# Second layer of a two-layer megakernel: three edits to its slot tables (decay loads, tile stores, the chain to the next batch's time steps)

## What is computed

```
xn = layernorm(x);  h = rmsnorm(xn)
u, z = split(h @ in_proj);  u = silu(conv4(u))
dt_r, B, C = split(u @ x_proj)
dt = softplus(dt_r @ dt_proj + b);  A = -exp(A_log)         # 256 channels x 16 states
state[t] = exp(dt[t] * A) * state[t-1] + dt[t] * B[t] * u[t]
y = (sum over states of C[t] * state[t] + u * D) * silu(z)
x + xn + y @ out_proj + (shared(xn) + top-2 of 8 experts(xn)) / 3
```

## Time and profile before

| | us |
|---|---|
| three runs | 1224.32, 1230.9, 1238.44 |
| their median | 1230.9 |
| profiled execution, its own time | 1228.28 |
| profiled execution, span from first to last instruction | 1226.5 |

### The profile page before, as it was taken

The page is one execution under the profiler, slowest core; times in us unless marked ns, Lnnn a source line. Parts: engine busy times, 40 slices in busy tenths (PEclk is TensorE's granted clock), DMA queues, the critical chain, the costliest instruction groups (busy, mean ns, idle before and its releaser), DMA issues. The chain is left out here.

```text
span 1226.5 us, 12808 instructions
## 1 busy us (share of the span) xinstructions
PE 871.2 (71%) x3620; PEld 412.1 (34%) x3620; DVE 938.6 (77%) x1280; ACT 505.5 (41%) x840; POOL 701.0 (57%) x427
## 2 busy tenths in 40 slices
PE   3668988888888656676587687688777688664552
PEld 0123333333333323344244344344434344311120
DVE  3467787977977445799469879688979779899973
ACT  0112212123123322473376386385495485663230
POOL 1021122031113561379569877569989879789996
PEclk9568788788897867699689899797999889875575
DMA  4886746666450352767766766767877767646631
GB/s 127 208 180 144 187 140 153 184 171 152 118 142 14 99 155 63 155 145 165 185 196 176 188 207 167 158 215 172 207 217 169 182 207 174 206 141 126 163 86 28
DMA packets 102849, 192.30 MB, mean 157 GB/s; under 512 B 13147, under 2 KB 68124, under 8 KB 90364
## 3 DMA queue, kind: packets, MB, share of 16 engines
q1 hardware_dynamic: 91516, 183.07, 57.2%
q0 software_dynamic: 11264, 8.43, 4.2%
HBM read 146.80 MB, written 32.06 MB: 146 GB/s over the span
## 5 line engine op out<-in xcount | busy, mean ns | idle before, releaser
L1681 POOL TENSOR_TENSOR hs<-hs,c_rep 128x1024 f32<-128x1024 f32 x128 | 332.0, 2604 | 87.7 <-DVE hs L1931 86.9
L1922 DVE TENSOR_TENSOR p_s_du<-p_s_du,b_rep 128x512 f32<-128x512 f32 x256 | 175.4, 685 | 49.5 <-PE p_s_du L2029 46.2
L2029 PE MATMUL p_s_du<-block_in,spread 96*128 96x512 bf16 x256 | 112.9, 442 | 115.5 <-DVE hs L1931 109.0
L1931 DVE TENSOR_TENSOR_SCAN hs<-decays,p_s_du 128x512 f32<-128x512 f32 x132 | 161.1, 1221 | 13.5 <-DVE p_s_du L1922 0.5
L1931 DVE TENSOR_TENSOR_SCAN hs<-slots,p_s_du 128x512 f32<-128x512 f32 x100 | 122.1, 1221 | 19.7 <-ACT slots L1826 9.7
L802 DVE TENSOR_TENSOR value_prod<-p_eb_y_acc,v 128x512 f32<-128x512 f32 x128 | 83.9, 685 | 56.6 <-PE p_eb_y_acc L1109 47.1
L513 POOL TENSOR_TENSOR sc<-ex,ex_part 128x1024 f32<-128x1024 f32 x8 | 17.0, 2129 | 171.6 <-ACT ex_part L619 171.6
L1826 ACT ACTIVATE decays<-decays,a_neg 128x512 f32<-128x512 f32 x132 | 91.7, 718 | 49.4 <-DMA decays<-dt_rows 39.3
L1720 POOL DMA_INDIRECT y_xr<-moe_sums,position x64 | 105.4, 1647 | 10.8 <-issue 8.2
L1686 POOL TENSOR_TENSOR y_hid<-y_hid,g_in 128x512 f32<-128x512 f32 x64 | 99.0, 1548 | 20.3 <-DVE y_hid L1944 19.8
L2029 PEld LDWEIGHTS p_s_du<-block_in,spread 96*128 96x128 bf16 x256 | 26.1, 102 | 249.4 <-DVE hs L1931 179.0
(11 more groups left out here) (193 smaller groups left out, 1751.6 us busy)
## 6 DMA issues: line engine op xcount, KB each, us to landing
decays<-dt_rows SPq DMA_DIRECT2D x33, 1024.0 KB
qb<-rq_rows SPq DMA_DIRECT2D x32, 1024.0 KB, 13.5
slots<-dt_rows SPq DMA_DIRECT2D x25, 1024.0 KB
wm<-in_wmoe SPq DMA_DIRECT2D x48, 384.0 KB
moe_rows<-zeros SPq DMA_DIRECT2D x8, 774.0 KB, 6.0
xg<-moe_rows SPq DMA_DIRECT2D x48, 129.0 KB
stack<-ex_part SPq DMA_DIRECT2D x96, 64.0 KB
block_in<-y_part SPq DMA_DIRECT2D x192, 32.0 KB
```

What stands on the lines that cost most here:

```text
L1681: nc.gpsimd.tensor_tensor(hs[:, n:n + 2], hs[:, n:n + 2], c_rep[p][:].unsqueeze(1).to_broadcast([128, 2, T]), ALU.mult)\
L1922: nc.vector.tensor_tensor(p_du[:, k % 2], p_du[:, k % 2], b_rep[p][:], ALU.mult).then_inc(dbu_done.sem, 1)
L1931: nc.vector.tensor_tensor_scan(hs[:, n % NA], home(8 * (b - 1) + k // 4)[:, bass.ts(j, T)], p_du[:, k % 2], 0.0, ALU.mult, ALU.add).then_i ...
L2029: nc.tensor.matmul(p_du[:, k % 2], spread[:, i], block_in[:, (2 * b + s) % NB, j], start=True, stop=True).then_inc(du_full.sem, 1)
```

## The change

Four things in the slot tables of layer 1; no instruction is added or taken away.

- SP, decay loads: from batch 2 on at slots 0, 4, 8, 12, 16 in place of 2, 6, 10, 14, 18 (q 3 to 7), and for the next batch at 22, 24, 28 in place of 22, 26, 30 (q 0 to 2). In a slot they now come first, then weights, then rows (before: rows, weights, decays).
- SP, tile stores: two slots later (`store`).
- The chain: `x_proj` to `third_part` one slot sooner on PE and ACT, two for `log_in`, `softplus_cut`, `softplus_end` and `steps`, one for `store_dt`, `stack` (first half) and the parts. On POOL `steps` comes ahead of `times_c` and `hidden` of its slot, and `hidden` ahead of `times_c`. `repeat_bc` goes from slot 16 to 19.
- The end of the batch before: `gather_y` of its last four slots from PE slot 3 to 2; `out_proj` from 9 to 13 and `result` from 11 to 15 (batches 2 to 7).

```diff
-  weigh=then + 6 if h else then + 2, store=then + 8 if h else then + 4),
+  weigh=then + 6 if h else then + 2, store=then + 10 if h else then + 6),
 # sync, batch
+                if b == 1 and k in (4, 8, 12, 15, 18):
+                    load_decays(1, {4: 3, 8: 4, 12: 5, 15: 6, 18: 7}[k])
+                if 1 < b <= B and k % 4 == 0 and k < 20:
+                    load_decays(b, (k + 12) // 4)
+                if nxt and k in (22, 24, 28):
+                    load_decays(b + 1, (k - 20) // 4)
+                (weights, then rows)
-                (rows, then weights)
-                if b == 1 and k in (4, 8, 12, 15, 18):
-                    load_decays(1, {4: 3, 8: 4, 12: 5, 15: 6, 18: 7}[k])
-                if 1 < b <= B and k % 4 == 2 and k < 20:
-                    load_decays(b, (k + 10) // 4)
-                if nxt and k % 4 == 2 and k > 20:
-                    load_decays(b + 1, (k - 22) // 4)
-                    if k == 16:
+                    if k == 19:
                         repeat_bc(b + 1, 1 - p)
-                    if k in (19, 21):
-                        store_dt(b + 1, (k - 19) // 2)
-                    if k in (21, 23, 24):
-                        stack(b + 1, 0, (21, 23, 24).index(k))
+                    if k in (18, 20):
+                        store_dt(b + 1, (k - 18) // 2)
+                    if k in (20, 22, 23):
+                        stack(b + 1, 0, (20, 22, 23).index(k))
 # gpsimd, batch: both now ahead of times_c
+                if nxt and k in (16, 18):
+                    steps(b + 1, q, (k - 16) // 2)
+                for _, _, j, v in due(b, k, "hidden"):
+                    hidden(v)
-                if nxt and k in (18, 20):
-                    steps(b + 1, q, (k - 18) // 2)
 # scalar, batch
-  copy_xd 9, dt_in 11 13, exp_z 13, one_more 14, log_in 15, first_part 20 23, second_part 22 25
+  copy_xd 8, dt_in 10 12, exp_z 12, one_more 13, log_in 13, first_part 19 22, second_part 21 24
 # vector, batch
-  result 11, softplus_cut 16, softplus_end 17, second_rest 21 24, third_part 22 26
+  result 15 if nxt else 11, softplus_cut 14, softplus_end 15, second_rest 20 23, third_part 21 25
 # tensor, batch
-  x_proj 8, dt_proj 10 12, last gather_y 3, out_proj(b - 1, 1) 9
+  x_proj 7, dt_proj 9 11, last gather_y 2, out_proj(b - 1, 1) 13 if nxt else 9
```

More of the change, by code:

```diff
@@ L1610, in batch @@
                         load_xr(0)
+                if b == 1 and k in (4, 8, 12, 15, 18):
[4 more added lines that the diff above has]
+                    load_decays(b + 1, (k - 20) // 4)
+                for _, _, j, _ in due(b, k, "weights"):
+                    if j is not None:
+                        load_weights(j)
                 for _, _, j, _ in due(b, k, "rows"):
@@ L1613, in batch @@
                         load_rows(j)
-                for _, _, j, _ in due(b, k, "weights"):
-                    if j is not None:
-                        load_weights(j)
-                if b == 1 and k in (4, 8, 12, 15, 18):
-                    load_decays(1, {4: 3, 8: 4, 12: 5, 15: 6, 18: 7}[k])
-                if 1 < b <= B and k % 4 == 2 and k < 20:
-                    load_decays(b, (k + 10) // 4)
                 if b == 4 and k == 30:
                     load_xr(1)
-                if nxt and k % 4 == 2 and k > 20:
-                    load_decays(b + 1, (k - 22) // 4)
                 for _, _, j, _ in due(b, k, "store"):
@@ L1735, in batch @@
                     times_c(b, p, k // 2 - 1)
-                for _, _, j, v in due(b, k, "hidden"):
-                    hidden(v)
                 if old and k == 5:
@@ L1874, in batch @@
                     silu_z(b + 1, q)
-                if k == 9:
+                if k == 8:
                     copy_xd(b + 1)
-                if k in (11, 13):
-                    dt_in(b + 1, (k - 11) // 2)
+                if k in (10, 12):
+                    dt_in(b + 1, (k - 10) // 2)
+                if k == 12:
+                    exp_z(b + 1)
                 if k == 13:
-                    exp_z(b + 1)
-                if k == 14:
                     one_more(b + 1)
-                if k == 15:
                     log_in(b + 1)
[L1885 to L1888, removed]
+                if k in (19, 22):
+                    first_part(b + 1, (k - 19) // 3)
+                if k in (21, 24):
+                    second_part(b + 1, (k - 21) // 3)
         def main(tail):
@@ L1966, in batch @@
                     skip(b - 1, q, 1)
-                if old and k == 11:
+                if old and k == (15 if nxt else 11):
                     result(b - 1)
@@ L1972, in batch @@
                     continue
-                if k == 16:
+                if k == 14:
                     softplus_cut(b + 1)
-                if k == 17:
+                if k == 15:
                     softplus_end(b + 1)
[L1977 to L1980, removed]
+                if k in (20, 23):
+                    second_rest(b + 1, (k - 20) // 3)
+                if k in (21, 25):
+                    third_part(b + 1, (k - 21) // 4)
         def main(tail):
@@ L2120, in batch @@
                 if nxt:
-                    if k == 8:
+                    if k == 7:
                         x_proj(b + 1, q)
-                    if k in (10, 12):
-                        dt_proj(b + 1, (k - 10) // 2)
+                    if k in (9, 11):
+                        dt_proj(b + 1, (k - 9) // 2)
                 if b + 2 <= B:
@@ L2132, in batch @@
                         gather_y(b, (k - 7) // 4)
-                if old and k == 3:
+                if old and k == 2:
                     gather_y(b - 1, GROUPS // 4 - 1)
-                if old and k == 9:
+                if old and k == (13 if nxt else 9):
                     out_proj(b - 1, 1)
```

## The result

The changed kernel takes 1271.9 us (median of 4 runs, 1268.3 to 1279.4) where the kernel before takes 1232.9 beside it (4 runs, 1224.3 to 1238.4). The ratio is 1.033, 95% interval 1.025 to 1.041: slower by about 39 us, where 1208 was forecast. Ratios in this document leave out executions that ran clearly slower than the fastest of the same kernel. The profiled execution takes 1270.29 us, its span is 1268.5.

What follows compares the result with a forecast made beforehand. DVE was taken to set the pace, losing 70.6 us to waits rooted in SP's late decay loads, with POOL setting the end. 1228.3 - 30 + 7 = 1205.3, plus 2.6 for the median: 1208 us, range 1192 to 1230.

Steps and rivals of the forecast that it cites:

- the part on the decay loads: SP's sooner decay loads remove the issue lag; rows and weights behind them stay covered; value between 0 and 70.6 us.
- The sentence on slot 24: SP: second-half `stack` waits behind scan 23, but is first read more than 20 slots later, so it costs nothing.
- 30 us gained: Of DVE's 70.6 us of waits up to slot 11 of batch 7, 30 us go; bounds 3 and 50.
- The cap: DMA rate in batches 2 to 6: 188 GB/s now, best batch 197; at 202 they take 31 us less.
- the lag of 7.55 us: SP, batch 5: q 2 may go when scan 27 ends, 861.18, but is issued at 868.73; claimed removed.
- The rival of full rings: Loads leave sooner but wait inside the DMA queue; 15 us go, 10 come back, 1226 us; chance 0.2.
- The rival on the slower side: The store takes 20.4 us, POOL's batch 7 fetch moves 14.4 us, sooner loads bring 3: 1245 us; chance 0.08.
- The store's term: Tile 47's store, behind a decay load in batch 7, delays POOL's first fetch and the end by 7 us.
- row for "no faster than 9.7 us": Profile row read as showing the 128 KB store lands no faster than 9.7 us, the median for `out`.
- The chain at nothing: PE, ACT and POOL steps moved sooner: gain inside the 30 us, price on ACT and POOL taken as nothing.
- The cost named, ACT late for slot 16: If ACT's moved chain work runs late, DVE waits for a decay near slot 16, up to 2 us a batch.
- Stores on SP: Later tile stores save SP's 50.0 us of waiting for `weigh`; that saving is counted in the decay loads.

Runs made afterwards that it cites:

- e9: The changed kernel with SP's tile stores first in every slot, ahead of decay loads, weights and rows; ratio to the kernel before 1.042 [1.036, 1.049].
- e3: The kernel before with only the sooner chain, the gather in slot 2 and `out_proj` in slot 13; ratio to the kernel before 1.011 [1.003, 1.018].
- e10: The kernel before with sooner chain, gather in slot 2, `out_proj` in 13, but POOL's old order inside a slot; ratio 1.010 [1.003, 1.017].
- e16: The changed kernel with loads of tile rows two slots sooner from batch 2 on, except tiles 24 and 25; ratio to the kernel before 1.060 [1.051, 1.068].

## Why the prediction was wrong

The step that failed is one clause of the part on the decay loads: rows and weights "stand eight slots ahead of their use, about 22 us, against landings of 17.2 us ...: covered, with little left". The 22 us were worked out from slots, not read from the issue. For most tiles they are right: in the trace of before PE is ready for rows some 25 us after their issue. But SP runs behind its slots towards the end of a batch, and for the second tile of each of batches 2 to 6 that time is 9.4 to 11.9 us. In the place above the rows left at 864.89 and PE was ready for them at 876.2 (878.63 less the wait of 2.45), a cover of 11.3 us against a landing of 13.7. Nothing was left of it. Then both ends got worse: in that place the issue stood behind eight stacks (9.65 us of SP's time) and the decay load, and the landing behind 1 MB more, 19.4 us in place of 13.7; the cover of these five tiles is 2.8 to 10.6 us in the changed kernel. The wait for a scan, which the prediction feared for rows, is not what held them. The sentence on slot 24 failed in the same way for the loads alone (45.0 us for stacks) though not in the full change, where the chain has the first stacks sooner. It looked at the stacks of the second half; what is late is late at the start of the next batch, so the first half is what it should have priced.

**The term "30 us gained" (bounds 3 and 50) has the wrong sign.** It was read as DVE's waits that stem from decays, capped by a rate. The cap was the right doubt, and too weak a one: the rate fell to 165 to 182 GB/s instead of rising to 202. A cap on the gain says nothing of whom the sooner load displaces. By the half loads, the loads' edit is worth 0 with room in the queue and -3.1% (38 us) without. Nor did the lag of 7.55 us go that the sum starts from: from scan 27 to the issue of q 2 it was 7.5 to 11.9 us in batches 3 to 6 before, and is 8.6 to 11.7 us now. The loads that did leave sooner are q 1 (6.9 to 13.6 us behind its scan before, 0.7 to 5.7 now), q 3 and q 7; q 5 and q 6 already left within 2 us of theirs.

**Why handing on costs.** Before, decays were late by 94.0 us for ACT, which works three slots ahead, and DVE lost 22.7 us to that directly. Now PE waits 54.8 us for rows, where it was 2.4 (11.4 for weights, where it was 9.6), and DVE waits 43.7 us more for its spread. PE holds the next spread behind the tile's transpose and has one slot of lead; the place above shows this once, that it explains the whole is argued. The prediction asked who waits for the load that is moved, and did not price the same lateness at those it is moved past.

**The rival of full rings** comes nearest to what the runs showed (loads wait inside a queue that has no room) and had chance 0.2, but was priced as "less gain", 1226. The rival on the slower side, 1245 at 0.07 for all that is slower, rested on POOL's fetch, and this was not what decided.

**The store's term was right for the fetch, too large for the end.** Forecast: fetch 7.0 us later against scan 11, bounds 3.7 and 11.2. Measured: 16.6 us after scan 11's end in place of 7.0, so 9.6 us, and the store landed 15.7 us after issue, above the 13 taken and under the 17.2 of the upper bound. The rule of the Trainium skill that put the price towards that bound (DMA: Bandwidth & Descriptors, Queues, rings and completion order) agrees with it as far as it goes: in e9, issued ahead of that load, the store landed after 12.5 us. The prediction's row for "no faster than 9.7 us" was that of another transfer, `out`; the tile stores of the kernel before landed after 5.8 us in the median. From the fetch to POOL's last product 130.2 us pass (131.6 before). Of the 9.6 us only 4 were to be had back in e9, where the fetch came 6.5 us sooner in its batch but 132.9 us passed behind it, so a delay of the fetch didn't move the end by as much.

**The chain at nothing was wrong by about 1%.** The cost named, ACT late for slot 16, did not show. PE's `x_proj` waits for ACT's silu instead, 23.2 us in e3, since it moved sooner while silu did not and silu stands behind late decays. In the full change, with decays in time, that wait is 6.4 us. `steps` ahead of `times_c` costs POOL a wait that gives 27.4 us in steady batches and is hidden there (e10 has the same ratio). At the end the chain does cost: batches 7 and 8 take 158.5 us in e3 and 157.2 in e10, and 153.4 to 156.3 in all eight profiles without it, so about half of the 9.5 us there is the chain's and not the store's. With half loads the full change is 1.0% slower than the kernel before, the chain and the end together.

**Stores on SP.** The wait for `weigh` did go, 50.0 to 0.3 us, and was worth nothing: with the later stores alone it was 19.7 us, and the ratio 1.011 (0.5% by the medians of all runs). Why that is over 1 stays open.

Of what was named to show the steps: ACT's wait under 45 us, right (32.1); the issue of q 2 within 1 us of scan 27, wrong (scan 27 of batch 4 ended at 864.0, the issue is at 873.73, since eight stacks took 9.65 us on SP); batches of 84 to 87 us, wrong; POOL's single wait, right. "If rows and weights come late for PE" is how it was said to fail, and is what happened.

**Open.** Why all eight loads together cost 3.1% where two and five cost 0.9 and 0.6: the place ahead of rows and weights was not tried without the new slots, and rows first brought back no more than 0.5%, within the intervals. Why the same lateness costs more in e16 than in the changed kernel. How much SP's waits for scans at slots 8 to 16 add to its being late at slot 28 when loads are whole: no run took them out and kept the loads' slots on SP. No version tried with whole loads is faster than the kernel before; the half loads show that some 40 us lie in the decays' bytes.

## What to carry to other kernels

When a load is moved forward in a queue that holds many microseconds of work, price the transfers that it passes, at the engine that waits for them: here no order of the whole loads brought a gain, and most brought a loss, as the engine that waited now had less lead than the one that waited before. Halving the bytes of the suspected load is a quick test of whether order or quantity is the limit; here it gave 3.3% at once, and no order did.

## What had not been expected of the hardware

- A DMA-issuing instruction on SP takes 0.36 to 0.66 us where it is short, and in the changed kernel's second layer up to 7.56 us for a decay load and up to 9.07 for a tile store. While it lasts SP issues nothing else. With half the bytes in the decay loads the instructions of over 1 us fall from 144.2 to 31.9 us in all, so the length goes with what is queued.
- Half of the bytes on a second queue, the same total: rows of 129 KB were waited for 111.5 us in place of 54.8. Whether the sizes of the packets, 7.7 KB in one queue and 1.0 KB in the other, are the reason was not tried.
- The mean busy share of the DMA engines is about the same without and with the change (0.68 to 0.76, 0.70 to 0.73 after), though the half loads show that the queue is what bounds: the mean share did not tell.
